# A Flamingo-style two-layer block on one core: small GpSimd work moved to VectorE and PE, rounding offsets taken off while leaving PSUM, two y buffers, new orders

## The reference, cut to what matters

```python
x = x + tanh(g_xattn[0]) * L0_xattn(ctx, ctx, layernorm(x))          # stage A
x = x + tanh(g_ffn[0])   * L0_ffn(layernorm(x))                      # stage M
x = x + tanh(g_xattn[1]) * L1_xattn(layernorm(x), ctx)               # stage F
x = x + tanh(g_ffn[1])   * L1_ffn(layernorm(x))                      # stage G
```

## Time and profile before

| | |
|---|---|
| runs | 399.1, 399.9, 401.47 us; median 399.9 |
| profiled execution | span 397.3 us, mean granted TensorE clock 0.948 |
| PE busy | 324.9 us, 82% |
| DVE busy | 313.1 us, 79% |
| POOL busy | 299.1 us, 75% |
| ACT busy | 256.4 us, 65% |
| DMA | 24.17 MB, mean 61 GB/s |

### The profile page before, as it was taken

How to read it: one execution, slowest core, us unless ns; L and a number is a source line. 1 busy time by engine, 2 the same in 40 slices (tenths; PEclk the granted TensorE clock), 3 DMA queues, 4 the chain that set the end, 5 groups by cost and what they waited for, 6 DMA issues and landing times.

```text
span 397.3 us, 10407 instructions
## 1 busy us (share of the span) xinstructions
PE 324.9 (82%) x3326; PEld 284.0 (71%) x3326; DVE 313.1 (79%) x913; ACT 256.4 (65%) x726; POOL 299.1 (75%) x459
## 2 busy tenths in 40 slices
PE   1365589898999789979998899879978997996875
PEld 1255469787898679867986698669957896994742
DVE  2679877598869997999799979995989678778434
ACT  4335254536846797779667885777658855875754
POOL 4378989799898989898999799988778873443010
PEclk9999767999999999999999999998999999999585
DMA  5967210300341114012401221204100000000000
GB/s 161 289 192 210 81 36 21 116 17 16 88 115 34 29 41 128 19 56 63 108 15 47 68 87 29 61 6 131 33 16 1 28 15 2 2 29 14 2 13 13
DMA packets 34454, 24.17 MB, mean 61 GB/s; under 512 B 3617, under 2 KB 32097, under 8 KB 34401
## 3 DMA queue, kind: packets, MB, share of 16 engines
q1 hardware_dynamic: 33680, 23.32, 19.7%
q10 hardware_dynamic: 720, 0.20, 0.2%
HBM read 16.16 MB, written 7.34 MB: 59 GB/s over the span
## 4 chain that ended last, share of the span: by engine, by line
PE 37%; POOL 25%; DVE 13%; issue 10%; ACT 7%; DMA 4%; SPq 3%; POOLq 0%; DVEq 0%; ACTq 0%
POOL tree L939 9%; PE ps_d L1448 8%; POOL attn L945 8%; PE ps_z L1188 4%; PE ps_a L1196 3%; PE ps_z L1189 3%; PE ps_z L1190 3%; POOL m_h L876 2%; DVE head_max L1584 2%; DMA wf_raw<-in_wd 2%; DVE m_u L1623 1%; DMA k_rows<-rows_dram 1%; DVE y L1655 1%; PE ps_sc L1234 1%; DVE shifted L1590 1%
## 5 line engine op out<-in xcount | busy, mean ns | idle before, releaser
L1188 PE MATMUL ps_z<-m_xhi,w_hi 128*128 128x256 f32 x240 | 76.9, 320 | 12.7 <-DVE m_h L1631 6.1
L945 POOL TENSOR_TENSOR attn<-attn,head_inv 128x1024 f32<-128x1024 f32 x32 | 75.8, 2371 | 0.2 <-DVE head_inv L1606 0.2
L1448 PE MATMUL ps_d<-wdn,m_h 128*128 128x128 f32 x512 | 71.4, 283 | 4.7 <-DVE m_h L1631 2.1
L1448 PEld LDWEIGHTS ps_d<-wdn,m_h 128*128 128x128 f32 x512 | 63.1, 194 | 8.5 <-issue 4.1
L1189 PE MATMUL ps_z<-m_xhi,w_lo 128*128 128x256 f32 x240 | 68.8, 287 | 0.0
L1190 PE MATMUL ps_z<-m_xlo,w_hi 128*128 128x256 f32 x240 | 68.6, 286 | 0.0
L1623 DVE SCALAR_TENSOR_TENSOR m_u<-m_tanh,ps_z 128x256 f32<-128x256 f32 x120 | 49.0, 411 | 17.6 <-ACT m_tanh L1033 16.7
L1033 ACT ACTIVATE m_tanh<-ps_z 128x256 f32<-128x256 f32 x120 | 45.9, 384 | 26.0 <-PE ps_z L1190 25.6
L1188 PEld LDWEIGHTS ps_z<-m_xhi,w_hi 128*128 128x128 f32 x240 | 46.7, 195 | 19.3 <-issue 6.1
L876 POOL TENSOR_TENSOR m_h<-m_u,m_z 128x256 f32<-128x256 f32 x56 | 41.1, 734 | 17.2 <-DVE m_u L1623 17.2
L939 POOL TENSOR_TENSOR tree<-tree 128x256 f32<-128x256 f32 (+2 forms) x90 | 46.4, 515 | 7.1
(11 more groups left out here) (311 smaller groups left out, 852.0 us busy)
## 6 DMA issues: line engine op xcount, KB each, us to landing
rows_dram<-qk_parts SPq DMA_DIRECT2D x16, 192.0 KB, 2.2
k_rows<-rows_dram SPq DMA_DIRECT2D x16, 192.0 KB
q_rows<-rows_dram SPq DMA_DIRECT2D x16, 192.0 KB
w_raw<-in_w SPq DMA_DIRECT2D x2, 1024.0 KB, 7.9
rows_dram<-qk_parts SPq DMA_DIRECT2D x16, 128.0 KB, 2.0
x_in<-in_x SPq DMA_DIRECT2D x8, 128.0 KB, 2.4
ct_in<-in_ctx_t SPq DMA_DIRECT2D x8, 128.0 KB, 2.4
rows_dram<-qk_parts SPq DMA_DIRECT2D x16, 64.0 KB, 1.7
```

The costliest lines, as they stand in the source:

```text
L945: pool.tensor_tensor(e, e, head_inv[:, u % 2].unsqueeze(1).to_broadcast([P, HEADS, HALF]), ALU.mult).then_inc(s_attn, 1)
L1188: pe.matmul(dst, hi_w, hi_x, start=start, stop=False)
L1448: last = pe.matmul(ps_d[:, b * P:(b + 1) * P], m_h[:, m % 4, b * P:(b + 1) * P], wdn[:, m], start=(k == 0), stop=(k == TPE - 1))
```

## The change

- `rstd` on GpSimd keeps only the power. VectorE adds eps before it (`dve.*_eps`, one 128x2 `tensor_scalar`) and makes minus mean times rstd after it (`dve.*_nmr`, one 128x2 `scalar_tensor_tensor`), as steps of their own in the order.
- `pool.top_probs` becomes four VectorE instructions in three steps (`dve.top_probs`); the comparison of expert numbers becomes one 128x32 instruction that no longer needs the probabilities (`dve.top_eq`), and the weights one 128x32 product where four 128x8 ones stood.
- b_l becomes a third row of `bias_parts`; PE adds it as one more bf16 matmul at the start of each of F's two output groups (`first_products`). `pool.y_res` and its buffer go. `bl` is loaded with the early small loads (`w_out`).
- `dve.g_q` and `act.g_pq` go. PE transposes the fp32 values with the offset still on; VectorE takes it off and clips while it reads PSUM (`dve.g_qt`, in the place of `act.g_qt`), and ScalarE takes it off in `act.g_pt`, which it ran before as a plain copy.
- Two `y` buffers, used by pairs in turn; the first GpSimd sum waits on the pair before the last one.
- Three set-up memsets on GpSimd go. All lists in `WHEN` and `ONCE` are new, loads and spare matmuls among them: `sp.w_ffn` moves ahead of `sp.w_out` and `sp.w_moe`.

```diff
-bias_raw = sb("bias_raw", [3 * QUAD, 2, P])
...
+bias_raw = sb("bias_raw", [3 * QUAD, 3, P])
...
-y = sb("y", [P, 2, P])
+ys = sb("y", [P, 2, 2, P])
...
-            for i, src in enumerate(("bv", "bo")):
+            for i, src in enumerate(("bv", "bo", "bl")):
...
-    def rstd(p, s_mv, s_rs, mv, rs):
-        pool.wait_ge(s_mv, p.count(2, 2))
-        pool.tensor_tensor(rs[:, 0], mv[:, :, 1], eps_col[:], ALU.add).then_inc(s_rs, 1)
-        pool.tensor_tensor(rs[:, 1], mv[:, :, 0], minus_ones[:], ALU.mult).then_inc(s_rs, 1)
-        pool.wait_ge(s_rs, p.count(4, 1))
-        pool.tensor_tensor(rs[:, 2], rs[:, 0], minus_half[:], ALU.pow).then_inc(s_rs, 1)
-        pool.wait_ge(s_rs, p.count(4, 3))
-        pool.tensor_tensor(rs[:, 3], rs[:, 2], rs[:, 1], ALU.mult).then_inc(s_rs, 1)
+    pool.wait_ge(c_misc, 5)
+    def rstd(p, s_rs, s_norm, rs):
+        pool.wait_ge(s_rs, p.count(3, 1))
+        wait(pool, s_norm, p.before().count(2, 2))
+        pool.tensor_tensor(rs[:, 0], rs[:, 2], minus_half[:], ALU.pow).then_inc(s_rs, 1)
...
-            rstd(p, s_mmv, s_mrs, m_mv, m_rs)
-        if p := due(now, "pool.top_probs"):
-            pool.wait_ge(s_texp, p.count(1, 1))
-            wait(pool, s_w12, p.before().count(4, 4))
-            pool.wait_ge(c_thh, 1)
-            pool.tensor_tensor(tsum[:], texp[:], ones[:, 0:2].unsqueeze(2), ALU.add).then_inc(s_tp, 1)
-            pool.tensor_tensor(texp[:], texp[:], th_half[:].unsqueeze(1).to_broadcast([P, 2, 1]),
-                               ALU.mult).then_inc(s_tp, 1)
-            pool.wait_ge(s_tp, p.count(5, 2))
-            pool.tensor_tensor(tsum[:], tsum[:], minus_one[:].unsqueeze(1).to_broadcast([P, 2, 1]),
-                               ALU.pow).then_inc(s_tp, 1)
-            pool.wait_ge(s_tp, p.count(5, 3))
-            pool.tensor_tensor(tprob[:, :, 0:1], th_half[:].unsqueeze(1).to_broadcast([P, 2, 1]), tsum[:],
-                               ALU.mult).then_inc(s_tp, 1)
-            pool.tensor_tensor(tprob[:, :, 1:2], texp[:], tsum[:], ALU.mult).then_inc(s_tp, 1)
...
-                    wait(pool, s_fyb, p.before().count(1, 1))
-                    wait(pool, s_fc, p.before().count(2, 2))
-                pool.tensor_tensor(y[:], y_raw[:, n], (y if n else x1)[:], ALU.add).then_inc(s_yp, 1)
+                    wait(pool, s_x3, p.before(2).count(1, 1))
+                    wait(pool, s_fc, p.before(2).count(2, 2))
+                pool.tensor_tensor(y(p), y_raw[:, n], y(p) if n else x1[:], ALU.add).then_inc(s_yp, 1)
...
-        if p := due(now, "pool.y_res"):
-            wait(pool, s_x3, p.before().count(1, 1))
-            pool.wait_ge(s_y, p.count(2 * DVE_SUMS, 2 * DVE_SUMS))
-            pool.wait_ge(c_thbo, 1)
-            pool.tensor_tensor(y_res[:], y[:], bl_all[:].unsqueeze(1).to_broadcast([P, 2, P]),
-                               ALU.add).then_inc(s_fyb, 1)
...
-        if p := due(now, "act.g_qt"):
-            wait(act, s_gu, p.before().count(4, 4))
-            for g in groups(p):
-                act.wait_ge(s_gqt, p.count(1, 1) + g[0])
-                act.activation(g_qt[:, cols(g)], batch_bank(p, g[0])[:, g[0] * HALF:(g[-1] + 1) * HALF].bitcast(BF16),
-                               ACT.Copy).then_inc(s_gqs, 1)
...
-                wait(act, s_gpq, p.before().count(2, b + 1))
+                wait(act, s_gpt, p.before().count(2, b + 1))
...
-            if p := due(now, "act.g_pq", b):
-                act.wait_ge(s_gpr, p.count(2, b + 1))
-                wait(act, s_gpt, p.before().count(2, 2))
-                act.activation(g_pq[:, b], g_pr[:, b], ACT.Copy, bias=-ROUND).then_inc(s_gpq, 1)
...
-                act.activation(g_pt[:, b], batch_bank(p, b)[:, 0:TOK].bitcast(BF16), ACT.Copy).then_inc(s_gpts, 1)
+                act.activation(g_pt[:, b], batch_bank(p, b)[:], ACT.Copy, bias=-ROUND).then_inc(s_gpts, 1)
...
+    def first_products(p, b):
+        s = slice(b * P, (b + 1) * P)
+        pe.matmul(late_bank(p, b)[:, s], ones_bf[:], bias_parts[:, 2], start=True, stop=False)
+        pe.matmul(late_bank(p, b)[:, s], f_ct[:, s], wl[:, 0], start=False, stop=False)
+        pe.matmul(late_bank(p, b)[:, s], f_c2q[:, s], wl[:, 1], start=False, stop=False)
...
-                pe.wait_ge(s_gq, p.count(1, 1) + g[0])
+                pe.wait_ge(s_gr, p.count(2, g[-1] + 1))
...
-                    last = pe.transpose(batch_bank(p, b)[:, b * HALF:(b + 1) * HALF].bitcast(BF16), g_q[:, b],
-                                        ident_bf[:])
+                    last = pe.transpose(batch_bank(p, b)[:, b * P:(b + 1) * P], g_r[:, b], ident[:])
...
-                pe.wait_ge(s_gpq, p.count(2, b + 1))
+                pe.wait_ge(s_gpr, p.count(2, b + 1))
...
-                    last = pe.transpose(batch_bank(p, b)[:, k * HALF:(k + 1) * HALF].bitcast(BF16),
-                                        g_pq[:, b, k * P:(k + 1) * P], ident_bf[:])
+                    last = pe.transpose(batch_bank(p, b)[:, k * P:(k + 1) * P],
+                                        g_pr[:, b, k * P:(k + 1) * P], ident[:])
...
+    def add_eps(p, mv, rs, s_mv, s_rs):
+        dve.wait_ge(s_mv, p.count(2, 2))
+        dve.tensor_scalar(rs[:, 2], mv[:, :, 1], EPS, None, ALU.add).then_inc(s_rs, 1)
+    def minus_mean_rstd(p, mv, rs, s_rs):
+        dve.wait_ge(s_rs, p.count(3, 2))
+        dve.scalar_tensor_tensor(rs[:, 1], mv[:, :, 0], -1.0, rs[:, 0], ALU.mult, ALU.mult).then_inc(s_rs, 1)
...
+        if p := due(now, "dve.top_eq"):
+            dve.wait_ge(s_tnof, p.count(1, 1))
+            dve.tensor_tensor(top_eq[:], expert_no[:].unsqueeze(1).unsqueeze(1).to_broadcast([P, 2, 2, EXPERTS]),
+                              top_nof[:, :, 0:2].unsqueeze(3).to_broadcast([P, 2, 2, EXPERTS]),
+                              ALU.is_equal).then_inc(s_teq, 1)
+        if p := due(now, "dve.top_probs", 0):
+            dve.wait_ge(s_texp, p.count(1, 1))
+            dve.tensor_scalar(tsum[:], texp[:], 1.0, None, ALU.add).then_inc(s_tp, 1)
+        if p := due(now, "dve.top_probs", 1):
+            dve.wait_ge(s_tp, p.count(4, 1))
+            dve.reciprocal(tinv[:], tsum[:]).then_inc(s_tp, 1)
+        if p := due(now, "dve.top_probs", 2):
+            dve.wait_ge(s_tp, p.count(4, 2))
+            if p.first:
+                dve.wait_ge(c_thh, 1)
+            dve.tensor_scalar(tprob[:, :, 0:1], tinv[:], th_half[:, 0:1], None, ALU.mult).then_inc(s_tp, 1)
+            dve.scalar_tensor_tensor(tprob[:, :, 1:2], texp[:], th_half[:, 0:1], tinv[:], ALU.mult,
+                                     ALU.mult).then_inc(s_tp, 1)
         if p := due(now, "dve.weights"):
-            dve.wait_ge(s_tp, p.count(5, 5))
-            dve.wait_ge(s_tnof, p.count(1, 1))
-            wait(dve, s_w, p.before().count(1, 1))
-            for b in range(2):
-                for k, dst in enumerate((w_first, w_second)):
-                    dve.tensor_scalar(dst[:, b], expert_no[:], top_nof[:, b, k:k + 1],
-                                      tprob[:, b, k:k + 1], ALU.is_equal, ALU.mult).then_inc(s_w12, 1)
+            dve.wait_ge(s_tp, p.count(4, 4))
+            dve.wait_ge(s_teq, p.count(1, 1))
+            dve.tensor_tensor(top_w[:], top_eq[:], tprob[:].unsqueeze(3).to_broadcast([P, 2, 2, EXPERTS]),
+                              ALU.mult).then_inc(s_w12, 1)
         if p := due(now, "dve.weights_sum"):
-            dve.wait_ge(s_w12, p.count(4, 4))
+            dve.wait_ge(s_w12, p.count(1, 1))
             wait(dve, s_y, p.before().count(2 * DVE_SUMS, 2 * DVE_SUMS))
-            dve.tensor_tensor(weights[:], w_first[:], w_second[:], ALU.add).then_inc(s_w, 1)
+            dve.tensor_tensor(weights[:], top_w[:, :, 0], top_w[:, :, 1], ALU.add).then_inc(s_w, 1)
         if p := due(now, "dve.a_xlo"):
...
-        if p := due(now, "dve.g_q"):
-            wait(dve, s_gqt, p.before().count(1, 1))
-            for g in groups(p):
-                dve.wait_ge(s_gr, p.count(2, g[-1] + 1))
-                dve.tensor_scalar(g_q[:, both(g)], g_r[:, both(g)], ROUND, 127.0, ALU.subtract,
-                                  ALU.min).then_inc(s_gq, 1)
+        if p := due(now, "dve.g_qt"):
+            wait(dve, s_gu, p.before().count(4, 4))
+            for g in groups(p):
+                dve.wait_ge(s_gqt, p.count(1, 1) + g[0])
+                dve.tensor_scalar(g_qt[:, cols(g)], batch_bank(p, g[0])[:, cols(g)], ROUND, 127.0, ALU.subtract,
+                                  ALU.min).then_inc(s_gqs, 1)
...
```

394 lines of the change are left out of this document (201 added, 193 removed), and 271 rows, old and new, of the table WHEN.

## The result

The changed kernel took 395.64 us (median of 13 runs, 392.75 to 399.93), the kernel before 399.31 us beside it (13 runs, 397.44 to 401.47). The ratio is 0.991 [0.988, 0.994]: faster by 1%, where 5.5% were forecast (377.9 us, range 369.5 to 390.5). The profiled execution spans 396.1 us, where the forecast span was 375.3.

What follows compares the result with a forecast made beforehand. GpSimd and VectorE, both about 90% busy, hold each other up; VectorE becomes the bound. From 397.3 us: -2.5 start, -12.5 middle, -2.5 next two, -4.5 last pair, -22 in all; plus 2.6 gives 377.9 us, range 369.5 to 390.5.

Steps and rivals of the forecast that it cites:

- The bound: In the five middle periods VectorE becomes the bound, above 93% busy; GpSimd busy near 262 us; a period 37 to 39 us.
- The price of VectorE's additions: Per pair on VectorE: 3.05 us added, 1.6 us removed, net +1.4 us, from +0.9 to +1.9; nothing charged for held steps.
- The place in between: Five middle periods: 37.9 us each, between 36.4 at best and 41.4 at worst; -2.5 us a period, -12.5 us in all.
- drains: Last 80 ns counted busy where VectorE then idles; some 16 gaps, 1.3 us a period, vanish when its queue closes up.
- Rival 2: VectorE bounds at today's share, so the five middle periods gain nothing; -9.5 us, 390.4 us; chance 0.15.
- What it frees is GpSimd's queue: The change releases 4.6 us a pair on GpSimd, which pays only where GpSimd is behind; the rstd chain gets no shorter.
- Rival 3: Product after the power waits behind GpSimd's large instruction, stalling VectorE's queue, 28 times 1.55 us: slower, 421 us; chance 0.05.
- The start: Up to 94.6 us: GpSimd's release and reordered loads, w_ffn first; -2.5 us, from 0 to -4.
- The two periods behind the middle: From 297.7 to 363.4 us: weights come sooner and G's chain loses two handovers; -2.5 us, from 0 to -5.
- The last pair: The last 33.9 us: G's roundings -0.5 and -0.3, new order -1.2, half clock -2.5; together -4.5 us, from -1 to -8.
- Rounding and bias: G's two roundings in the last pair: -0.5 and -0.3 us; bias: y_res's 0.73 us a pair leaves GpSimd for two PE matmuls.

Runs made afterwards that it cites:

- e5: e4 plus scratch products on GpSimd that nobody waits for, about as much work as the change takes off it; ratio 1.012 to the kernel before.
- e4: The changed kernel with the order of the kernel before up to 52.7 us, spare matmuls included; 394.24 us, ratio 0.990 to the kernel before.
- e7: e4 with the five small steps of the routing probabilities back on GpSimd; ratio 0.999 to the kernel before.
- e13: e4 with all four small steps of each normalisation back on GpSimd; ratio 0.982 to the kernel before.
- e15: e4 with both the routing probabilities and the normalisations' small steps back on GpSimd; ratio 0.991 to the kernel before.
- e2: The new code in the orders of the kernel before, new small VectorE steps placed; 436.9 us, ratio 1.082 to the kernel before.
- e3: The code of the kernel before in the changed kernel's orders; 428.1 us, ratio 1.073 to the kernel before.
- e12: e4 with the old rounding of the last FFN put back in the new order; 414.4 us, ratio 1.043 to the kernel before.
- e1: The changed kernel with VectorE's rounding of the FFN weights moved behind GpSimd's w_lo; ratio 0.986 to the kernel before.
- e16: e4 with the spare matmuls of the last pair doubled, in F and in G; ratio 0.989 to the kernel before.
- e14: e4 with the third-stage bias added on GpSimd again; ratio 0.991 to the kernel before.
- e6: e4 plus one scratch bn_stats of 128x128 on VectorE ahead of each product of minus mean and power; ratio 1.007 to the kernel before.

## Why the prediction was wrong, point by point

- **The bound.** Right: VectorE became it, with 94% of the middle (above 93% was forecast), and GpSimd's sum was near (266.3 us for 262). The middle periods are 39.5 us, outside the 37 to 39.
- **The price of VectorE's additions** was mis-sized: +1.4 us a pair by the nearest rows, +2.3 measured (18.3 / 8, with the start's roundings 0.5 of it). The sum had the earlier trace rows before it, worked out that such steps could add 1.3 us a pair, and charged nothing, for steps "which the order can set into gaps". This step of the sum failed. The order did so for some (M's product: 132 ns) and not for others: the mean of the second probability is 585 ns for 202. The weights' rounding, with one SBUF tensor in, was held too, 5.46 us for 1.4. The Trainium skill (SBUF — State Buffer, "Who interferes with whom") names `tensor_scalar` among the forms that can contend with GpSimd, and the trace agrees; I had taken only the part on two inputs.
- **The place in between** failed too. I put VectorE at 96% of a sum from which 1.3 us of drains had gone, because "afterwards only one is near full". It ran at 94% of 37.2 us. Against five periods of 37.9 us, 8.2 us are missing: 3.8 from the work (0.75 x 5) and 4.5 from 0.9 us more idle time a period. The table has 7.1, since the sum took its 2.5 us off a period of 40.4 us, the mean of three, and all five have 40.6. The same slip is in VectorE's base, where 36.3 us is the mean of the three full periods. The kernel before over all five:

```profile
94.60:297.70 203.10, 179.54 (x1923) 159.55 (x1920) 175.89 (x531) 147.53 (x430) 181.50 (x275) 0.99 0.20 57
```

  That is 35.2 us a period. So VectorE's work rose by 2.0 us a period, not 1.4, and only because the base was 1.1 too high does the forecast 37.7, before drains, lie above the measured 37.2. (GpSimd's 91.4% of the three periods is 91.3.) e5 shows the flaw in "only one": GpSimd at 69% still costs 0.3 us for each us. Rival 2 (today's share of VectorE, 390.4 us) was the nearest, and still too fast.
- **"What it frees is GpSimd's queue".** This step failed as an account. The square of e4, e7, e13 and e15 shows that the release of 3.9 us a pair, paid with VectorE steps, nets nothing, +0.9% and -0.8%. I said that "the rstd chain gets no shorter", and took the two handovers added as free; e13 shows that the handovers and VectorE's added work together cost more than GpSimd's release of 2.4 us a pair was worth. How much of it is the handovers isn't shown.
- **Rival 3** had the right mechanism, a step of 0.2 us in a full queue for which others stand, with a chance of 0.05. In the changed kernel the order avoids it (M's product 132 ns). In e2 it is there as I described it, 1.0 us a product of M, up to 2.25, and 12.1 us of ScalarE's waiting, and e3 and e12 (11.9 and 11.8 us of TensorE's for `g_q`) show the like for another step; these kernels are 4 to 8% over the kernel before. The price I gave it, 421 us, is of that size, though no run has it alone.
- **The start** had the wrong sign: +5.6 us for -2.5. I looked at the loads' order and not at what stood beside what. In the profile VectorE's roundings and GpSimd's `w_lo` collide at 18.8 us, and TensorE's clock is at 1.2 GHz for 44 us. With the order of the kernel before (e4) the start is 3.7 us shorter in the profile; with the collision alone taken away (e1) it is not. The profiled execution is 2.3 us over the median, so part of the 5.6 may be that one execution's.
- **The two periods behind the middle**: -2.5 forecast, +1.0 measured. I had named TensorE as nearest to full there and then charged it nothing. It is busy 62.9 us in them, 60.3 before, and 33.9 of 35.7 in the first. The fp32 transposes are 0.5 us a pair dearer, as forecast (13.4 us in all for 9.4 by the groups), but here on the engine that is nearest to full; the bias products of F, charged at nothing, are another 16 matmuls of 0.2 us.
- **The last pair**: -4.5 forecast, -2.4 measured. The clock in it is 0.82, up from 0.70, not 1.00, and a held clock seems worth less than the 2.5 us that I counted for half of it: e16 went from 0.70 to 1.00 in a stretch of F and won 0.4 us there. The added spare matmuls cost it 2.7 us in G, since they stand in front of the real ones.
- **Rounding and bias.** The bias at nothing was right (e14). The rounding at 0.8 us can't be judged: the edit is worth 5.3% in the new order and -0.7% in the old. The prediction priced the edits one by one, as if the orders would fit any of them.

What stays open is what the 0.9% of e15 comes from, how the edits would do in an order made for them from the old one, why the routing steps gain 3.7 us where the rates of e5 and e6 give nothing, and one `y` buffer instead of two, which wasn't tried, since the new order starts the next pair's sum before the last one is read.

## What to carry to other kernels

Where each engine's order is written out, code and order are one thing: price a change of code at the place that each step gets, and don't undo or test half of it in the other's order, for it looked like 5 to 8% here. Moving small steps from a full engine to one as full went either way here (+0.9% and -0.8%), so try each such move alone; a step of 0.2 us in the middle of a chain can be held 2 us, with the queue behind it. When the trace shows once that a step is held three times its length, put that into the sum. And count the spare matmuls that stand ahead of a real one, for it waits for all of them.

## What the runs showed of the hardware

- A 128x2 VectorE step with its inputs in SBUF, 0.21 us at best, lasted up to 1.32 us beside GpSimd's tree sum, and ended within 0.05 us of it; in e2 one lasted 2.25 us beside GpSimd's `attn` of 2.35. On average the second probability took 2.8 times its shortest (585 ns for 209).
- A step with one SBUF tensor in is held too: three VectorE roundings of 128x512 took 5.46 us beside two GpSimd differences of 128x1024, and 0.48 us each without them, while GpSimd's pair took 5.12 us with and 4.67 without (e1); a `g_q` of 128x256, 399 ns on average in the kernel before, lasted 2.31 us beside GpSimd's `attn` in e12.
- TensorE's granted clock went to 1.2 GHz at 26 us inside a gap of 3.1 us and also, in e1, at 27 us, at the end of the second of two gaps of 1.0 and 0.9 us, with half of the time between 24 and 28 us idle. It came back only at 70 us, though TensorE was busy 18.8 of the first 30.8 us and 11.9 of the next 13.6. In e4, with the spare matmuls and all else of the start in the old places, it was 0.91 from 26 to 44 us and 0.84 from 26 to 70.
- A clock of 1.00 for 0.70 shortened the last stage F by 0.4 us of 8.5, while seven and eight more spare matmuls ahead of real ones cost 1.8 and 0.95 us in G (e16 against e4).
